# Column sums of the kept diagonal chunks: f32 matmuls of 32 columns on TensorE in place of VectorE additions

## What is computed

```python
def _L0_gnn_ref(X, adj, W, b):
    adj_hat = adj + jnp.eye(adj.shape[0])
    d_inv_sqrt = 1.0 / jnp.sqrt(jnp.sum(adj_hat, axis=1))
    adj_norm = adj_hat * d_inv_sqrt[:, None] * d_inv_sqrt[None, :]
    return relu(adj_norm @ (X @ W) + b)

def _L1_gnn_ref(x, adj, weight, self_weight):
    support = x @ weight
    output = relu(support + adj @ support + x @ self_weight)
    return pair_norm(output)

x = layernorm(x + _L0_gnn_ref(x, adj, W, b))
x = layernorm(x + _L1_gnn_ref(x, adj, weight, self_weight))
```

## Time and profile before

| | |
|---|---|
| median of 3 runs | 1867.64 us |
| profiled execution | 1867.01 us |
| its span (first to last instruction) | 1865.2 us |
| PE busy | 1665.8 us (89%) |
| DVE busy | 1450.2 us (78%) |
| ACT busy | 1201.5 us (64%) |
| read from and written to memory | 570.68 MB, 306 GB/s over the span |
| mean granted TensorE clock | 0.961 of full speed |

### The profile page before, as it was taken

One profiled execution on the slowest core, in us unless ns is written; L12 is line 12 of the kernel. 1 busy time (PEld: TensorE's weight loads), 2 busy tenths in 40 slices (PEclk: granted clock), 3 DMA queues, 4 the chain that ended last, 5 costly groups with the idle time before them and its releaser, 6 DMA issues.

```text
span 1865.2 us, 20558 instructions
## 1 busy us (share of the span) xinstructions
PE 1665.8 (89%) x7682; PEld 1253.5 (67%) x7682; DVE 1450.2 (78%) x1893; ACT 1201.5 (64%) x1636; POOL 21.2 (1%) x42
## 2 busy tenths in 40 slices
PE   1087898998998999889999999999989999999993
PEld 0054565555555666677788888888868888877872
DVE  4476687796888789976767665665599999999997
ACT  3576686777756656645554454454468888888875
POOL 0000000000000000100000000000000000000001
PEclk7589999999999999999999999999999999999995
DMA  9999999999999668844444445545589999999943
GB/s 398 422 421 421 421 396 422 397 411 398 384 380 419 238 267 361 317 157 167 171 169 172 179 180 185 191 169 201 188 330 385 385 387 385 388 375 368 387 185 90
DMA packets 87459, 572.03 MB, mean 307 GB/s; under 512 B 8960, under 2 KB 17152, under 8 KB 19264
## 3 DMA queue, kind: packets, MB, share of 16 engines
q1 hardware_dynamic: 84928, 562.07, 76.8%
q0 software_dynamic: 2432, 8.65, 1.3%
HBM read 566.49 MB, written 4.19 MB: 306 GB/s over the span
## 4 chain that ended last, share of the span: by engine, by line
PE 64%; DVE 16%; DMA 11%; ACT 5%; issue 3%; SPq 0%; ACTq 0%; DVEq 0%
PE acc L1033 17%; PE acc L1035 16%; PE acc L1039 16%; DVE raw_low L724 6%; DMA s<-in_adjN 4%; DMA raw<-in_adjT 3%; DMA zr<-in_adjT 3%; PE pC L1013 3%; ACT hi L550 2%; DVE s L744 2%; DVE o_low L724 2%; PE pA L1033 1%; DVE zr_low L724 1%; PE pB L1033 1%; PE pB L1039 1%
## 5 line engine op out<-in xcount | busy, mean ns | idle before, releaser
L1033 PE MATMUL acc<-hi,rhi 128*128 128x512 f32 x1792 | 728.9, 407 | 65.4 <-DVE raw_low L724 43.9
L724 DVE TENSOR_TENSOR raw_low<-raw,hi 128x1024 fp32r<-128x1024 f32 x558 | 662.2, 1221 | 70.2 <-ACT hi L550 65.0
L550 ACT ACTIVATE hi<-raw 128x1024 fp32r<-128x1024 f32 x558 | 573.1, 1054 | 165.4 <-DMA raw<-in_adjT 73.2
L1035 PE MATMUL acc<-raw_low,rhi 128*128 128x512 f32 x1520 | 597.6, 393 | 0.0
L1039 PE MATMUL acc<-hi,rlo 128*128 128x512 f32 x1792 | 556.8, 392 | 0.0
L1033 PEld LDWEIGHTS acc<-hi,rhi 128*128 128x128 f32 x1792 | 339.1, 189 | 244.8 <-DVE raw_low L724 118.6
L1039 PEld LDWEIGHTS acc<-hi,rlo 128*128 128x128 f32 x1792 | 339.3, 189 | 73.7
L1035 PEld LDWEIGHTS acc<-raw_low,rhi 128*128 128x128 f32 x1520 | 288.0, 189 | 58.4 <-issue 3.3
L550 ACT ACTIVATE hi<-zr 128x1024 fp32r<-128x1024 f32 x158 | 164.4, 1058 | 47.7 <-PE acc L1039 23.5
L723 DVE TENSOR_TENSOR rlo<-zr,rhi 128x256 fp32r<-128x256 f32 x123 | 52.1, 423 | 171.7 <-ACT hi L550 171.7
L544 ACT ACTIVATE rhi<-zr 128x256 fp32r<-128x256 f32 x123 | 50.8, 413 | 191.7 <-PE acc L1039 191.7
(11 more groups left out here) (186 smaller groups left out, 1612.3 us busy)
## 6 DMA issues: line engine op xcount, KB each, us to landing
raw<-in_adjT SPq DMA_DIRECT2D x279, 1024.0 KB, 5.7
zr<-in_adjT SPq DMA_DIRECT2D x79, 1024.0 KB, 6.6
raw<-in_adjN SPq DMA_DIRECT2D x54, 1024.0 KB, 16.6
o<-in_adjT SPq DMA_DIRECT2D x32, 1024.0 KB, 11.2
s<-in_adjN SPq DMA_DIRECT2D x30, 1024.0 KB, 17.0
s<-in_adjT SPq DMA_DIRECT2D x30, 1024.0 KB, 13.9
zr<-in_adjN SPq DMA_DIRECT2D x28, 1024.0 KB, 19.2
s<-in_xT POOLq DMA_DIRECT2D x8, 512.0 KB, 7.6
```

The source lines that it names most:

```text
L550: S.activation(hi[n % DEEP][:, :], slice_of(chunk, j), ACT.Copy).then_inc(hi_ready, 1)
L724: V.tensor_sub(low_of(chunk, j), slice_of(chunk, j), hi[n % DEEP][:, :].bitcast(f32)).then_inc(slice_split, 1)
L1033: T.matmul(banks[h][:, :], a, hi[n % DEEP][:, part], start=opens, stop=False, skip_group_check=True)
L1035: T.matmul(banks[h][:, :], a, low_of(chunk, j)[:, part], start=False, stop=False, skip_group_check=True)
```

## The change

`sum_kept` goes, with its 56 additions, the buffer `colsum` and the semaphore `col_step`. `close_sums(k)` calls `add_sums` for each of the four kept chunks of row k instead of the two matmuls of 128 columns. The two banks of `sums` are set to zero by VectorE at the start, since no matmul opens them any more. The place of the close in TensorE's order, the kept chunks' loads and their place in SyncE's order stay.

```diff
+    kept_chunks = [[c for c in chunks if c.kind == "keep" and c.row == k] for k in range(NB)]
...
             V.memset(pick[:, :].bitcast(f32), 0.0).then_inc(pick_zero, 1)
+            for h in range(H):
+                V.memset(sums[h][:, :], 0.0).then_inc(sums_zero, 1)
...
-            def sum_kept(chunk):
-                k, q = chunk.row, chunk.q
-                dve.wait_ge(*landed(chunk))
-                if q == 0:
-                    if k > 0:
-                        dve.wait_ge(sums_closed, k)
-                    V.tensor_add(colsum, slice_of(chunk, 0), slice_of(chunk, 1)).then_inc(col_step, 1)
-                    return
-                for j in range(JB):
-                    dve.wait_ge(col_step, k * (JB * Q - 1) + q * JB + j - 1)
-                    V.tensor_add(colsum, colsum, slice_of(chunk, j)).then_inc(col_step, 1)
...
                 if chunk.kind == "keep":
-                    sum_kept(chunk)
                     continue
...
                 for t in range(JB * H):
                     j, h = t // H, t % H
-                    T.matmul(sums[h][t * QUARTER:(t + 1) * QUARTER, :], to,
-                             slice_of(chunk, j)[:, h * HALF:(h + 1) * HALF], start=False, stop=False,
-                             skip_group_check=True)
+                    last = T.matmul(sums[h][t * QUARTER:(t + 1) * QUARTER, :], to,
+                                    slice_of(chunk, j)[:, h * HALF:(h + 1) * HALF], start=False,
+                                    stop=chunk.kind == "keep" and chunk.q == Q - 1, skip_group_check=True)
+                return last
...
             def close_sums(k):
-                pe.wait_ge(col_step, (k + 1) * (JB * Q - 1))
-                to = pick[:, NB - 1 - k:NB - 1 - k + P].bitcast(f32)
-                for h in range(H):
-                    last = T.matmul(sums[h][:, :], to, colsum[:, h * HALF:(h + 1) * HALF],
-                                    start=(k == 0), stop=True, skip_group_check=True)
+                for chunk in kept_chunks[k]:
+                    last = add_sums(chunk)
                 last.then_inc(sums_closed, 1)
                 closed[0] = k + 1
...
+            pe.wait_ge(sums_zero, H)
             close_sums(0)
```

More of the change, by code:

```diff
@@ L352, in graph_kernel @@
         xT_blk = s1[:, 0:BLK]
-        colsum = s1[:, BLK:2 * BLK]
         rsum = [s1[:, 2 * BLK + r * NB * BG:2 * BLK + (r + 1) * NB * BG] for r in range(2)]
@@ L393, in graph_kernel @@
         dve_summed = sem("dve_summed")
-        col_step = sem("col_step")
+        sums_zero = sem("sums_zero")
         sums_closed = sem("sums_closed")
```

## The result

The changed kernel took 1873.7 us (median of 7 runs, 1872.56 to 1876.59) beside 1867.85 us for the kernel before (7 runs, 1866.3 to 1870.15): ratio 1.0034, 95% interval 1.0022 to 1.0046, so slower by 0.34%. Forecast were 1876.2 us and a range of 1868.5 to 1883.5 us.

A forecast was written before the change was run, and what follows sets the result against it. Loads bound stages 1 and 2, with their share falling in stages 5 to 7 as VectorE gets busy. Closes cost 14.0 us, missing additions return 5.4: +8.6 us, forecast 1876.2 us, range 1868.5 to 1883.5 us.

The forecast's parts named there:

- Extra of a close: TensorE at each close: four kept chunks take 3.75 us instead of 1.73, 2.0 us extra a stage, between 1.9 and 3.0.
- The width rival: Every chunk of the close pays the change of width: extra 3.0 us a close, +15.6 us, 1883.2 us; chance 0.12.
- On the path in each stage: Closes of stages 1 to 7: each 2.0 us extra delays the rest in full, 14.0 us; stage 0 costs nothing.
- Give-back: Missing additions on VectorE return 0.35, 3.3, 1.4 and 0.35 us in stages 4 to 7, 5.4 us; stages 1 to 3 nothing.
- next to be late: Last product before the close, stages 4 and 6: once VectorE is earlier, the load limits the gain to 0.35 and 1.4 us.
- the terms for stages 4 and 6: Last product before these closes: VectorE starts earlier without the additions, giving back 0.35 us and 1.4 us.
- The end: Stage ends later by about 2, 4, 6, 7.7, 6.4, 7.0 and 8.6 us; behind stage 7 the rest moves as a whole.
- Loads hide the extra: Rival for stages 1 to 3: only four closes cost, +2.6 us, 1870.2 us; chance 0.13.
- VectorE is the bound of stages 5 to 7: Rival: all 8.5 us of additions a stage on the path there, 11.9 us less, 1855.7 us; chance 0.07.
- The clock: Rival: TensorE's clock falls one or two more times where TensorE is the bound, 1878.8 to 1881.4 us; chance 0.08.

The follow-up runs named there:

- again: The changed kernel once more, unaltered, beside the kernel before: 1875.43 us, ratio 1.0037; its profiled execution took 1872.03 us.
- my first two attempts at a better kernel: spread and inline: three or all four kept chunks' matmuls moved from the close to ahead of earlier products; 1865.4 and 1876.07 us.
- gain: Kernel before without the additions, close left at two f32 matmuls of 128 columns (sums of seven slices left out): 1862.68 us, ratio 0.9973.
- early: The change in stages 1 to 3 alone, other stages as in the kernel before: 1872.82 us, ratio 1.0024.
- double: As early, with four more narrow groups, multiplied by zeros, at each of its three closes: 1884.31 us, ratio 1.0089.
- cost: The changed kernel's longer close, with the additions of the kernel before kept but unused: 1881.33 us, ratio 1.0066.
- inline: Changed kernel with all four kept chunks' groups sent ahead of products in stages 1 to 7, none at the close: 1876.07 us, ratio 1.0045.
- spread: Changed kernel with three of four kept chunks' groups sent ahead of products in stages 1 to 7, one at the close: 1865.4 us, ratio 0.9989.
- inline_t1: inline with the copy of the banks one product earlier in ScalarE's order: 1860.74 us, ratio 0.9962 to the kernel before.
- filled: inline with two narrow groups multiplied by zeros (1.73 us) at the close, ScalarE waiting for them: 1873.02 us, ratio 1.0027 to the kernel before.
- one: Changed kernel with only the fourth kept chunk's group at the close of stages 1 to 7 (others' sums left out): 1860.42 us, ratio 0.996.

## Why the prediction was right, point by point

- *Extra of a close: 2.0 us forecast, 1.87 measured* (stage 1 above; stages 6 and 7 of again give 6.66 us from product to copy against 4.77 and 4.78). The step was 4 x 0.90 + 0.15. The passes follow at 0.43 us and not 0.45, and from the last product to the first narrow multiplication it is 2.95 us against 2.87, so the way in costs 0.08 us. The width rival, 1.19 us a chunk, falls: there is no gap between groups of one width. The Trainium skill, "TensorEngine Tiling (Array Packing)", Key Properties, says that a change of the tiling mode, and not only of the tile, drains TensorE. The trace agrees, with no gap inside one width and 0.08 us at the change.
- *On the path in each stage: right, but with a reason that was only half seen.* Rows of stage 1 in again and double move by the whole extra. What I had not asked is how much of the old close was on the path. The chain of waits runs through it, which I read as 1.73 us of path, and the row of ScalarE above shows 0.19 us of wait. That it didn't hurt the forecast was luck: only the difference above the old length entered, and the old length was just about the hidden one. It ruined my first two attempts at a better kernel.
- *Give-back: 5.4 us forecast, 5.0 measured with gain (3.2 to 7.1 by its interval).* The split over stages was off, and that the total came out near was luck in its parts. TensorE's idle time before products in again, against the kernel before:

```profile
579.12 0.50 PE L1023 MATMUL acc<-hi,rhi 128*128 128x512 f32 x1 [0.65 <-DVE o_low L726]
583.41 0.50 PE L1023 MATMUL acc<-hi,rhi 128*128 128x512 f32 x1 [1.27 <-DVE o_low L726]
...
670.52 0.50 PE L1023 MATMUL acc<-hi,rhi 128*128 128x512 f32 x1 [0.43 <-DVE raw_low L726]
...
732.02 0.50 PE L1023 MATMUL acc<-hi,rhi 128*128 128x512 f32 x1 [0.19 <-DVE raw_low L726]
```

In stage 5 the 2.02, 0.66 and 0.66 us of the earlier trace rows are gone, as forecast. Rows of the kernel before that I hadn't counted:

```profile
565.82 0.50 PE L1033 MATMUL acc<-hi,rhi 128*128 128x512 f32 x1 [0.48 <-DVE o_low L724]
572.30 0.50 PE L1033 MATMUL acc<-hi,rhi 128*128 128x512 f32 x1 [0.75 <-DVE o_low L724]
...
727.08 0.50 PE L1033 MATMUL acc<-hi,rhi 128*128 128x512 f32 x1 [1.65 <-DVE raw_low L724]
```

The first of them goes too, and the second shrinks to 0.65: 3.9 us in all by the idle rows, 4.4 by the milestone (1.87 + 2.51), where I had 3.3. In stage 7 I gave back 0.35 us, from VectorE's start against the data. The idle time of TensorE before the last product fell from 0.20 + 1.65 to 0.19 us, and the copy came only 0.16 us later than at the close before, in place of 2.0 - 0.35 = 1.65. In stage 6 I gave back 1.4 us and it was 0.4 (1.87 - 1.48). Stages 6 and 7 together are 2.1 us against my 1.75: the load that I called "next to be late" isn't fixed. It waits for buffers that products free, and it came 1.0 us later in stage 6 and 1.4 us earlier in stage 7, counted from the close before. Stage 4 gave back nothing that can be seen.

  gain shows what the additions alone are worth, with the old close in place: by its milestones 3.0 us in stage 5, nothing in stages 4 and 6 beyond 0.2 us, and 0.3 us in stage 7, where TensorE still waits before the last product:

```profile
724.75 0.50 PE L1023 MATMUL acc<-hi,rhi 128*128 128x512 f32 x1 [1.66 <-DVE raw_low L726]
```

  So the terms for stages 4 and 6 don't show, and what again saves in stage 7 it saves only together with the longer close. gain's profiled execution is 2.3 us under that of before at stage 7, with 1.2 us lost in stage 3, where its clock falls (0.79 from 419 to 427 us); the rest up to the 5.0 us of the medians is not settled.
- *The end.* At stage 7 again is 6.8 and the changed kernel 9.3 us later, around the forecast 8.6. Of the 2.5 us between these two executions of one kernel 1.8 arise in stage 3, where the clock falls in one of them, 0.4 before it, and 0.5 in stage 6, where it falls in neither. A window of stage 3 in the changed kernel:

```profile
426.00:434.00 8.00, 8.00 (x29) 5.02 (x28) 3.97 (x6) 6.92 (x12) 0.00 (x0) 0.67 1.02 425
```

and one in again:

```profile
429.00:437.00 8.00, 6.43 (x30) 4.33 (x31) 5.28 (x6) 6.66 (x11) 0.00 (x0) 1.00 1.02 421
```

0.33 x 8 = 2.6 us of work are missing in the first. By the two ratios the change costs 6.4 and 6.9 us, 1.7 to 2.2 less than forecast: 0.9 us are the smaller close (7 x 0.13), the rest is about the size of what two executions of one kernel differ by, and is not settled.
- *Rivals.* Loads hide the extra: against, by early and double for stages 1 to 3, and by cost less early for the rest. VectorE is the bound of stages 5 to 7: against, since gain removed the additions and won 5.0 us, not 26. The clock: it falls behind no close of the changed kernel, where TensorE waits 1.30 us; inline and spread show that it can. But it fell once in stage 3 of the changed kernel's execution and once in stage 4 of again (0.79 from 518 to 526 us), where the execution of before has no fall. The forecast had it that a fall where loads are the bound costs nothing; the 1.8 us of stage 3 speak against that. How much of the median is due to such falls stays open.

What stays open: the copy moved to tail 1 in the kernel before was not tried. By the rows it could gain nothing at the copy, which there waits 0.16 to 0.66 us for the close already.

## What to carry to other kernels

Before you price a longer or shorter step at a hand-over, look at the engine that takes over and at the instruction just ahead of the receiving one: if that ends within a few tenths of the hand-over, making the step longer costs in full and making it shorter gains next to nothing until the other side is moved too. Here the groups sent ahead without the moved copy gained 2.1 us (spread) or lost 8.4 (inline), and together with it they gave the fastest version, 7.1 us under the kernel before. Work sent ahead is free only in stages where its engine waits for something else; count its idle rows stage by stage before you move it.

## What the runs showed of the hardware that was not expected

- At the closes of stages 1 to 5 of six kernels (before, spread, inline, inline_t1, filled and one) TensorE waits for the copy 30 times. Behind the 24 waits of 1.27 to 1.73 us the granted clock stays at 1.00; behind the six of 2.12 to 2.71 us (five in inline, one in spread) it falls to 1.2 GHz for a while, which takes 1.7 us of work. Idle time of TensorE can be dearer than it looks. The length of the wait alone doesn't decide it, though. At the close of stage 6 inline waits 2.21 us, as long as at that of stage 5, and the clock stays:

```profile
680.57 0.59 PE L1007 MATMUL pC<-raw,pick 128*32 128x512 f32 x1 [2.21 <-ACT t L569]
...
680.00:688.00 8.00, 7.43 (x39) 4.58 (x40) 3.16 (x3) 3.28 (x4) 0.00 (x0) 1.00 0.62 226
```

  And behind stage 7 the same wait ahead of a product leaves the clock alone in before (the first two rows) and not in again (the last two):

```profile
777.70 0.50 PE L1033 MATMUL acc<-hi,rhi 128*128 128x512 f32 x1 [2.65 <-DVE raw_low L724]
...
777.00:785.00 8.00, 6.57 (x31) 5.22 (x32) 7.69 (x15) 5.53 (x9) 0.00 (x0) 1.00 1.01 419
...
784.68 0.50 PE L1023 MATMUL acc<-hi,rhi 128*128 128x512 f32 x1 [2.67 <-DVE raw_low L726]
...
784.00:792.00 8.00, 7.32 (x27) 5.93 (x28) 7.69 (x15) 5.60 (x9) 0.00 (x0) 0.79 0.93 368
```

- Two spans of the changed kernel differ by 4.4 us (1874.6 and 1870.2), with the same instructions: 2.5 us up to the close of stage 7 and 1.9 behind it. A single execution says little about an effect of 0.3%. The milestone at the first close repeats within 0.1 us (218.29, 218.30 and 218.32 in the changed kernel, again and early), but at the third it already differs by 2.1 us between the first two, so the later columns of the table are to be read with such an error.
